# One core, attention with a gated recurrence and an expert layer: thirteen TensorE waits taken out, the start and the orders of all engines rewritten

## The reference

```python
def reference(x, cond_1024, ...):            # x: 32 x 128 x 128, cond: 32 x 128
    x = x + attn(cond_attn(x, cond))         # both with 16 heads of 8
    x = x + ffn(cond2(x, cond))
    return x
# cond_attn: q = x Wq + bq; one key and one value row per batch from cond;
#            softmax over the 16 heads, context, output projection
# attn:      softmax of q over the 8 dims; k = elu(k) + 1; linear attention,
#            summed up over HEADS by cumsum; output projection
# cond2:     for each of 128 steps: [hidden, out] = sigmoid([x_t, h] W + b)
#            m = x_t Wx + bx + hidden * (h Wh + bh); h = out*h + (1-out)*tanh(m)
# ffn:       router logits of 8 experts, the best 2 kept (softmax of the two);
#            square(relu(h W1[e])) W2[e], summed with the two weights
```

## Time and profile before

| | us |
|---|---|
| median of 3 runs | 382.89 (381.85 to 383.90) |
| profiled execution, its own time | 382.63 |
| its span from first to last instruction | 380.9 |
| TensorE busy in it | 364.9 (96%) |
| VectorE | 321.5 (84%) |
| ScalarE | 297.1 (78%) |
| GpSimd | 261.9 (69%) |

### The profile page before, as it was taken

How to read it: one execution, slowest core, us unless ns; L and a number is a source line. 1 busy time by engine, 2 the same in 40 slices (tenths; PEclk the granted TensorE clock), 3 DMA queues, 4 the chain that set the end, 5 groups by cost and what they waited for, 6 DMA issues and landing times.

```text
span 380.9 us, 9218 instructions
## 1 busy us (share of the span) xinstructions
PE 364.9 (96%) x2522; PEld 306.4 (80%) x2522; DVE 321.5 (84%) x1159; ACT 297.1 (78%) x1136; POOL 261.9 (69%) x273
## 2 busy tenths in 40 slices
PE   4899999899999999999999999999999999999985
PEld 3588887677888888888888888888888888888864
DVE  2367998899999999999999999999999999997430
ACT  3455534458999899999999989999998899887774
POOL 4699523797777777777777777777877777784000
PEclk9999999999999999999999999999999999999999
DMA  7600000000000000000000000000000000000000
GB/s 197 232 2 0 3 0 3 0 3 0 9 8 9 9 7 9 8 9 9 9 9 8 9 9 11 10 11 8 9 9 8 9 9 9 9 9 9 9 9 14
DMA packets 7587, 6.78 MB, mean 18 GB/s; under 512 B 880, under 2 KB 6256, under 8 KB 7536
## 3 DMA queue, kind: packets, MB, share of 16 engines
q1 hardware_dynamic: 7104, 5.79, 5.0%
q10 hardware_dynamic: 432, 0.39, 0.4%
HBM read 4.09 MB, written 2.10 MB: 16 GB/s over the span
## 4 chain that ended last, share of the span: by engine, by line
PE 79%; DVE 10%; issue 6%; ACT 3%; DMA 1%; POOL 0%; SPq 0%; DVEq 0%; ACTq 0%; POOLq 0%
PE bank L385 70%; PE bank L538 7%; DVE kvs L1101 2%; PE bank L487 1%; PE bank L475 1%; DMA cwv<-in_cwv_dram 1%; DVE CTX L1031 1%; DVE h L1161 1%; ACT hid L848 1%; PE bank L427 1%; DVE rden L1093 1%; DVE mem L1141 1%; DVE att L1110 1%; DVE bank L1153 1%; ACT hsq L856 0%
## 5 line engine op out<-in xcount | busy, mean ns | idle before, releaser
L343 POOL TENSOR_TENSOR qc<-kvs,qn 128x512 f32<-128x512 f32 x64 | 81.4, 1273 | 15.8 <-DVE kvs L1101 11.7
L385 PEld LDWEIGHTS bank<-h,gwh 128*128 128x128 f32 x512 | 69.0, 190 | 20.0 <-DVE h L1161 18.0
L848 ACT ACTIVATE hid<-bank,gw 128x128 f32<-128x128 f32 x256 | 80.0, 372 | 4.2 <-PE bank L385 0.2
L331 POOL TENSOR_TENSOR kv<-kv,qkv 128x512 f32<-128x512 f32 x64 | 81.2, 1270 | 2.5
L1101 DVE TENSOR_TENSOR_SCAN kvs<-bank,kv 128x256 f32<-128x256 f32 x128 | 81.2, 657 | 0.2
L385 PE MATMUL bank<-h,gwh 128*128 128x32 f32 x512 | 71.0, 262 | 1.5 <-DVE h L1161 1.4
L385 PE MATMUL bank<-w,hsq 128*128 128x128 f32 x512 | 69.7, 279 | 1.8 <-ACT hsq L856 1.8
L385 PE MATMUL bank<-w,h 128*128 128x512 f32 x128 | 66.1, 598 | 0.0
L385 PEld LDWEIGHTS bank<-w,hsq 128*128 128x128 f32 x512 | 62.4, 192 | 3.6 <-ACT hsq L856 3.6
L385 PE MATMUL bank<-h,whw 128*128 128x64 f32 x256 | 53.0, 289 | 0.0
L875 ACT ACTIVATE gt<-bank 128x64 f32<-128x64 f32 x128 | 29.4, 230 | 24.4 <-PE bank L385 24.1
(11 more groups left out here) (113 smaller groups left out, 749.3 us busy)
## 6 DMA issues: line engine op xcount, KB each, us to landing
out_dram<-res SPq DMA_DIRECT2D x32, 64.0 KB
XT<-in_x_t_dram SPq DMA_DIRECT2D x7, 256.0 KB, 6.4
w<-in_w_dram SPq DMA_DIRECT2D x2, 512.0 KB, 5.5
XT<-in_x_t_dram ACTq DMA_DIRECT2D x1, 256.0 KB, 3.9
aw<-in_aw_dram SPq DMA_DIRECT2D x1, 192.0 KB, 3.2
gwx<-in_gw_dram SPq DMA_DIRECT2D x1, 128.0 KB, 5.0
gwh<-in_gw_dram SPq DMA_DIRECT2D x1, 128.0 KB, 4.3
cwk<-in_cwk_dram ACTq DMA_DIRECT2D x1, 64.0 KB, 1.8
```

Of the source, the lines that this page charges most:

```text
L331: pool.tensor_tensor(kv[:, a * D:b * D, :].rearrange("p (d e) h -> p d e h", d=D // 2), kv[:, D * D + a:D * D + b, :].unsqueeze(2).broadca ...
L343: pool.tensor_tensor(qc[:, a:b, :, :], kvs[:, a * D:b * D, :].rearrange("p (d e) h -> p d e h", d=D // 2), qn[:, p, a:b, :].unsqueeze(2).b ...
L385: return pe.matmul(dst, w, rhs, start=start, stop=True, skip_group_check=True)
L848: last = act.activation(hid[:, half, j, :], hidden_bank(t, half)[:, j * DE:(j + 1) * DE], ACT.Relu, scale=gw[:, p, NE - 1 - e:NE - e])
```

## The change

**Waits.** Thirteen `wait_ge` of TensorE go: `aT_sb` and `xr_ok` in `att_T`; `xb_ok` and `xr_ok` in `project_out`; `x1_done` and `aT_sb` in `x_rows`; `zb_ok` in `gates_x`; `x1_done` in `memory_x`; `hsq_sb` in `logits`; `h_done` in `hidden`; `hsq_sb` in `hidden_T`; `xr_ok` and `x1_done` in `experts_out`. In the loop some TensorE instructions waited for three semaphores, now nearly all wait for one.

**ScalarE's order.** In an iteration `att_out(t+1)` now stands behind `x1_bias(t+1)`, `square(t-1, 0)` before the last `gates`, and `x_rows_out(t-1)` at the end, behind both halves of `relu(t-1, 1, ..)`, which stood at the head of the next iteration.

**TensorE's order.** `x_rows(t-2)` moves from before `step_gates(t - 1, 3)` to behind `memory_x(t)`; `hidden(t-1, 0)` and `experts_out(t-2, 0)` change places; `experts_out(t-2, 1)` goes before `att_T`. The finale has another order too.

**Start.** cwk and cwv go out first on SP with the second part of x behind them; condT and cols go on ScalarE's queue. EARLY is 8, so the keys of the first two units come out of the first product; VectorE builds the key blocks of unit 1 that GpSimd built. TensorE begins with four, then three more products of `ident` whose result nobody reads. The combined weights (`cwoT` with `aw`) are made after the first scores. VectorE's mask of the scans is written in the loop of the units.

**Ramps and VectorE's, GpSimd's loops** are in another order throughout. Of the two finales in the diff the first is TensorE's, the second ScalarE's.

```diff
-EARLY = 4
+EARLY = 8
...
-        KV = [(condT[:, :], cond_t), (cols[:, :], cols_d), (cwv[:, :], cwv_d)]
-        KEYS = [(cwk[:, :], cwk_d)]
+        KV = [(cwk[:, :], cwk_d), (cwv[:, :], cwv_d)]
+        COND = [(condT[:, :], cond_t), (cols[:, :], cols_d)]
...
+            pe.wait_ge(ident_ok, 1)
+            warm(4)
             pe.wait_ge(w_kv, KV_ALL)
...
+            warm(3)
             pe.wait_ge(consts, 1)
             pe.wait_ge(kvm, 1)
             mm(keys_early, rep_d[:, :], kmask[:, :, 0:EARLY]).then_inc(kr_ps, 1)
...
             def project_out(t):
                 pe.wait_ge(aT_sb, t + 1)
-                pe.wait_ge(xb_ok, t + 1)
-                at_least(pe, xr_ok, t - 1)
...
             key_blocks(dve, 0, 2, 0).then_inc(kbd0_ok, 1)
+            key_blocks(dve, GROUP, GROUP, 0).then_inc(kbd0_ok, 1)
             largest(0)
...
             def finale():
+                x_rows(30, 0)
                 x_rows(31, 1)
+                logits(31, 1)
+                hidden_T(30, 1)
                 experts_out(30, 0)
-                logits(31, 1)
+                experts_out(30, 1)
                 hidden(31, 1, 0)
-                hidden_T(30, 1)
-                experts_out(30, 1)
                 hidden_T(31, 0)
                 hidden(31, 1, 1)
                 experts_out(31, 0)
...
             def finale():
-                relu(30, 0, 1, 0)
-                relu(30, 0, 1, 1)
                 gate_exp(31, 1)
-                relu(31, 1, 0, 0)
+                taken_sum(31, 1)
                 square(30, 1)
-                relu(31, 1, 0, 1)
-                taken_sum(31, 1)
                 finish(30, 0)
                 x_rows_out(31)
+                relu(31, 1, 0, 0)
+                relu(31, 1, 0, 1)
                 square(31, 0)
```

More of the change, by code:

```diff
@@ L392, in q_of, with warm @@
                 mm(bank[7][:, :], cwq[:, :], XT[:, GROUP * g:GROUP * (g + 1), :].rearrange("p b s -> p (b s)")).then_inc(q_ps, 1)
+            def warm(n):
+                for _ in range(n):
+                    mm(MEM[:, 0:P], ident[:, :], ident[:, :])
+            pe.wait_ge(ident_ok, 1)
+            warm(4)
             pe.wait_ge(w_kv, KV_ALL)
@@ L646, in ramp @@
                 step_memory(2, 0, 0)
-                experts_out(0, 0)
+                hidden(1, 1, 0)
                 hidden_T(0, 1)
@@ L666, in iteration @@
                 if has(0):
-                    gates_x(t, p)
                     memory_x(t, p)
+                if has(-2):
+                    x_rows(t - 2, p)
+                if has(0):
                     step_gates(t, p, 0)
@@ L673, in iteration @@
                     step_memory(t, p, 0)
+                if has(-1):
+                    hidden(t - 1, q, 0)
                 if has(-2):
-                    experts_out(t - 2, 0)
                     hidden_T(t - 2, 1)
@@ L681, in iteration @@
                     qkv_of(t + 4)
-                if has(-1):
-                    hidden(t - 1, q, 0)
+                if has(-2):
+                    experts_out(t - 2, 0)
                 if has(0):
@@ L956, in iteration @@
                     x1_bias(t + 1)
+                    att_out(t + 1)
                 if has(-1):
-                    x_rows_out(t - 1)
+                    square(t - 1, 0)
                 if has(0):
@@ L1211, in ramp @@
                 sum_heads(1, 1)
-                divisors(1)
-                inverses(1, 0)
-                inverses(1, 1)
+                add_dims(0, 0)
+                add_dims(0, 1)
                 head_max(2, 0)
```

264 lines of the change are left out of this document (124 added, 140 removed).

## The result

The changed kernel takes 387.40 us (median of four runs, 385.22 to 388.89) where the kernel before took 382.61 (381.85 to 383.90) beside it. The ratio is 1.0117, with a 95% interval of 1.0061 to 1.0174. The forecast of 382.4 was wrong, and the time lies 0.4 above the end of its range: the change makes the kernel 1.2% slower.

The account below looks back on a forecast made before the run. TensorE was taken as nearly full, ScalarE's row setting the next tile's start. Start -1.6, stage-one end -1.5, first tiles +0.3, end +2.3 sum to -0.5 from 382.63; plus 0.26 for the median: 382.4 us, range 377.6 to 387.0.

Parts of the forecast that it names:

- Start: Up to unit 1's scores: cwv lands 1.2 us earlier and a hole closes; -1.6 us, between 0 and -2.9.
- the hole before unit 1: TensorE's 0.70 us wait for GpSimd's key blocks before unit 1's scores; goes, with -0.4 of it counted.
- Rival C: Start brings nothing, by the transfer rule or x's first part landing later; +2.4, so 384.8 us; chance 0.07.
- End of stage one: Last normalise to first gates_x: earlier qkv bias and reordered VectorE and GpSimd work; -1.5 us, between +0.3 and -2.6.
- the 1.2 us of divisors and inverses: VectorE's tile 1 work moved before stage one's last normalise; most of the 1.2 us was to find a hole.
- The loop: 28 tiles: 0.03 us gained at gates_x, 0.03 lost at expert products; tile stays 9.25, total 0, bounds ±4.2 us.
- the old hole: TensorE's wait before the projection for ScalarE's x_rows_out: 0.19 us a tile, 0.23 with the slow first pass; closes.
- the row of hand-overs: Last tile's end: logits, drop_others, transposes, square and products in order before hidden(31, 0); +2.3 us, +1.7 to +2.9.
- the first tiles: First loop tiles, whose queues are not yet filled, cost +0.3 us.
- Waits costed at 0: TensorE's removed waits were fulfilled earlier than the one that stays, so their removal gains 0.
- A: Loop gets TensorE's own pace, tile 9.10 to 9.16; 378.2 to 379.9, taken as 379.0 us; chance 0.33.
- B: ScalarE holds the next tile at gates_x, x1_out behind att_out and square; tile 9.37 to 9.40, 386.4 us; chance 0.22.

Follow-up runs that it names:

- e7: Kernel before, order untouched, with nine of the thirteen TensorE waits taken out; 382.89 us, ratio 1.0000.
- e13: e8 with another order of first transfers: cwk, cwv, cwq, aw, cwoT, x part 1 on SP; condT, cols, x part 0 on ScalarE's queue; 379.49 us.
- e14: e8 measured again, beside e13 on the same chip; 380.91 us, ratio 0.9937.
- e15: e13 unchanged, measured again; 379.69 us, ratio 0.9918.
- e8: Kernel after with old finale order, fills in tile 1 and x_rows ahead of gates_x together; 380.68 us, ratio 0.9940.
- e6: Kernel after with the old start: old transfers, EARLY = 4, GpSimd's key blocks, no warm products; 385.64 us, ratio 1.0098.
- e3: Kernel after with the transpose x_rows moved ahead of the next tile's gates_x in TensorE's loop; 384.45 us, ratio 1.0036.
- e9: Kernel after with 20 more already fulfilled waits at VectorE's start; 386.77 us, one execution.
- e1: Kernel after with the old order of the finale, loop untouched; 384.27 us, ratio 1.0016.
- e4: Kernel after with twelve of the thirteen TensorE waits put back, all but project_out's xr_ok; 388.85 us, ratio 1.0143.
- e5: Kernel after unchanged, measured once more; 387.84 us, ratio 1.0118.
- e2: Kernel after with six short products that nobody reads put into the gaps of tile 1 of the ramp; 386.19 us, ratio 1.0091.
- e10: Kernel after with 40 more already fulfilled waits at VectorE's start; 390.02 us, one execution.
- e12: Kernel after with old finale order and x_rows ahead of gates_x, without fills in tile 1; 381.19 us, ratio 0.9962.

## Why the prediction was wrong, point by point

**Start: the step failed.** cwv did land earlier, by 0.9 and not 1.2, and the hole before unit 1 did go. The step that failed took the landing of cwv as what sets the first scores. The same edit put the first part of x third behind condT and cols and cwq on ScalarE's queue and laid x's second part beside it, and TensorE then waits for that. Rival C named this ("x's first part lands later behind three others") and got 0.07; it was the case. Its 2.4 us is not what "brings nothing" comes to, which is 1.6, so 384.0. The prediction costed the transfer that the chain showed and not the next one behind it. Of the +0.28, about 0.2 is the rise of the clock, 0.45 us later than in the kernel before (an estimate from before and e7, where a rise 0.97 later put unit 1 back by 0.40). With both transfers in time the start of e13 is worth 1.4 us against the changed one, side by side (e13, e14), and 0.8 by the ratios of e15 and e8, which ran apart. That is near the forecast's 1.6, but an unknown part of it comes from the earlier rise.

The Trainium skill ("DMA: Bandwidth & Descriptors", Issuing engines are not separate DMA queues) says that transfers from all issuing engines run on the same DMA engines and interleave. The trace agrees: x part 0 was issued 0.5 us later and landed 1.8 later (7.4 against 5.6), with 256 KB more under way, issued ahead of it on the other engine's queue. The prediction had made of it that a landing moves by about one issue; cwv moved by 0.9 where its issue moved by 0.46, and x part 0 by more than three times its issue.

**End of stage one: right sign, too small.** 2.26 us gained, forecast 1.5. e6, with the old start and this ramp, has the same 55.1 us from unit 1 to the first gates_x, so it is the ramp's. How much of the 1.2 us of divisors and inverses that I set against the gains was hidden wasn't tried. The lower bound of -2.6 had no term behind it: the two gains named add up to 1.8, less than what came.

**The loop: one term missing, two right.** x1_out followed gates_bias by 0.32 (forecast 0.31), gates_x came 3.98 behind the third gate product (4.00). The failing step is "TensorE then has one transpose more (0.11) before the next gate product": it is 0.11 and 0.10 more, because the first load of gates_x now waits for x1_out and lies open in front of the second pass. Before, only the projection had such a load; after the change both have (the projection's second pass comes 0.18 behind its first before and 0.21 after). So closing the hole in front of the projection did not take the price of its open load away, and gates_x has that price as well. The 0.10, less the 0.02 by which gates_x came before its forecast, makes an ordinary tile 0.08 longer, 9.35 against 9.27, some 2.2 us over 28 tiles. (The 0.23 us a tile that the prediction gives for the old hole is 0.26 by its own terms, 0.19 and 0.46 - 0.39; its forecast doesn't rest on that.) The Trainium skill ("TensorE: Matmul & The Clock Gate", Step-by-step: what each phase is for) has the load pulled ahead of the product that is still running; the trace agrees for passes whose load has nothing to wait for, 0.11 apart, and shows 0.21 behind a load that waits. e3 covers the load of gates_x with a transpose, its ordinary tile is back at 9.27, and it gets 2.04 us back of 2.91. The other 0.9 are the long tiles (1.33 against 0.43): not in the forecast at all. One execution of e9, which only adds waits at VectorE's start, has 28 tiles that are 0.83 shorter.

**The end: the row of hand-overs was right, +2.35 against +2.3** (24.58 in e3, 24.76 in e6, forecast "about 24.5"). What was missing is the clock: 1.8 us more in an execution where it falls. I had read "in the last 22.23 us only in 16.70" and not asked what longer waits do to the rate of what follows.

**Tile 1 of the ramp:** forecast +0.3 for the first tiles. Without the fall the first three tiles take 26.98 (e1) against 27.37, 0.4 less; with it 28.60, so 1.6 more than without. The edit that took the fill out of tile 1 was in the diff and got no line in the prediction: its cost stood at nothing without a reason.

Together: +0.28 - 2.26 - 0.39 + 1.62 (clock) + 2.91 + 2.35 + 1.79 (clock) = +6.30, the difference of the two spans. More than half of it, 3.4 us, is the clock. By their mean clock seven of the eight executions of the kernel after have at least one of the two falls, five of them both. The sum is that of the profiled execution, the longest; between the medians (387.40 and 382.61) lie 4.79 us.

**Waits costed at 0: right.** e7 (ratio 1.0000) and the 28 tiles of e4 (+0.23 us for twelve) agree. Twelve of the thirteen waits that the change is named after are worth nothing that can be measured. The thirteenth, `xr_ok` of `project_out`, stood in the hole of 0.19 us a tile, and it is gone only together with the new orders; what those cost is the rest of this section.

**Rivals.** A (379.0) fell. B had the right side, the right place (gates_x behind x1_out) and nearly the time (386.4), but in part by luck: its tile was 9.37 to 9.40, and 9.37 came as a mean, yet the fourth gates and x1_out came only 0.05 and 0.07 us behind the forecast's places, where B wanted 0.14 of delay at x1_out. It was the open load, the long tiles and the clock that made up the time.

## What to carry to other kernels

A wait that is long fulfilled cost nothing here (0.1 us in 28 tiles): don't give up a good order to be rid of it. A product whose own weight load has to wait costs more than the wait, since its next pass comes 0.10 us late as well; a short product without a wait in front of it hides that (0.07 us a tile here, 2 us in all). When an order takes work away from TensorE where it waits for others anyway, keep products that nobody reads in the gaps, and judge a kernel by several executions with their granted clock, since a fall shows in some only. And when a transfer is pulled forward, look at what lands last after it, not at what landed last before.

## What the runs showed of the hardware

- The same first 75 us of program met a clock that rose at 5.9, 11.1, 12.2, 12.6, 13.0 and 13.8 us (e1, after, e8, e5, e3, e2), and the first scores of unit 1 started between 13.5 and 16.2 with it. In tile 1 it fell behind TensorE's waits in five of the nine profiles without fills there (after, e4, e9, e10, e12; not in e1, e3, e5, e6), and in none of the eight with the fills of e2. Under the end of the kernel after it fell in five of eight profiles (after, e2, e4, e5, e10; not in e3, e6, e9), under the end of before in none of eleven.
- VectorE and ScalarE stand still for 0.2 to 0.35 us at fixed places of the program, some 22 us apart, with a packet of the instruction queue 0.65 to 0.89 us behind. Across chips and executions of one kernel they are the same tiles. Where such a place falls on the row of the recurrence, the tile is longer by 0.05 to 0.36 us; elsewhere it is free.
- A gates_x whose first load waited for ScalarE took 0.55 us for four passes (after), 0.46 behind a short transpose (e3), 0.45 where the load was done under the product ahead (before).
